# Four decoder blocks on one core: tiles of maxima one or two steps later in each attention, layer norm statistics in two halves

## What is computed

```python
x = x + _L0_xattn_ref(...)          # kernel phase 0
x = x + _L0_ffn_ref(...)            # 1
x = x + _L1_xattn_ref(ctx, ctx, _layernorm(x), mask, Wv, Wk, Wq)      # 2, 16 heads of 16
x = x + _L1_ffn_ref(...)            # 3
x = x + _L2_xattn_ref(_layernorm(x), ctx, ctx, mask, wq, bq, ...)     # 4, 16 heads of 16
x = x + _L2_ffn_ref(...)            # 5
x = x + _L3_xattn_ref(_layernorm(x), ctx, ctx, Wqkv, ..., 32)         # 6, 32 heads of 8
x = x + _L3_ffn_ref(...)            # 7

def _layernorm(x, axis=-1, eps=1e-05):
    return (x - mean(x)) / sqrt(var(x) + eps)

attn = softmax(where(mask == 0, -1e20, q @ k.T / sqrt(EMBED)))        # one head
out = attn @ v
```

## Time and profile before

| | us |
|---|---|
| median of 3 executions | 1696.71 (1695.7 to 1700.76) |
| the profiled execution | 1700.49 |
| its span | 1698.0 |
| TensorE matmul busy | 1474.7 (87%) |
| VectorE busy | 1025.1 (60%) |
| ScalarE busy | 755.2 (44%) |
| GpSimd busy | 116.4 (7%) |

### The profile page before, as it was taken

The page is one execution under the profiler, slowest core; times in us unless marked ns, Lnnn a source line. Parts: engine busy times, 40 slices in busy tenths (PEclk is TensorE's granted clock), DMA queues, the critical chain, the costliest instruction groups (busy, mean ns, idle before and its releaser), DMA issues.

```text
span 1698.0 us, 27047 instructions
## 1 busy us (share of the span) xinstructions
PE 1474.7 (87%) x9938; PEld 1099.3 (65%) x9945; DVE 1025.1 (60%) x2263; ACT 755.2 (44%) x1259; POOL 116.4 (7%) x168
## 2 busy tenths in 40 slices
PE   6999999878879895799889999999997989999456
PEld 4666666556774443477767778787773777778345
DVE  3455564778877764687756162433428888886334
ACT  2222112257764565476752212222214867788223
POOL 1000000000000000111000000000010011010423
PEclk9999999999998997899989999999998999999679
DMA  9451101310000000000009700000100000000176
GB/s 322 140 198 62 62 0 62 135 44 13 13 2 1 1 1 1 24 13 14 2 27 348 237 27 2 2 2 2 32 8 6 1 7 2 7 2 2 45 259 228
DMA packets 59540, 99.82 MB, mean 59 GB/s; under 512 B 10739, under 2 KB 48748, under 8 KB 59246
## 3 DMA queue, kind: packets, MB, share of 16 engines
q1 hardware_dynamic: 57022, 82.57, 14.9%
q10 hardware_dynamic: 512, 11.11, 1.9%
q0 software_dynamic: 1872, 4.27, 0.7%
HBM read 76.23 MB, written 38.35 MB: 67 GB/s over the span
## 4 chain that ended last, share of the span: by engine, by line
PE 49%; issue 22%; DVE 13%; ACT 6%; DVEq 4%; DMA 2%; SPq 2%; ACTq 1%; POOLq 1%; POOL 1%
PE bank L1969 7%; PE bank L1970 7%; PE bank L1645 6%; PE bank L1662 5%; PE bank L2028 3%; PE bank L1768 2%; PE bank L1819 2%; DVE MB L912 2%; DVE plo L930 2%; DMA jx<-copy_routed 2%; PE bank L1739 1%; DVEq L1199 1%; ACT e L1399 1%; PE bank L1741 1%; PE bank L1773 1%
## 5 line engine op out<-in xcount | busy, mean ns | idle before, releaser
L930 DVE TENSOR_TENSOR plo<-e,phi 120x512 f16<-120x512 f32 x256 | 179.7, 707 | 52.1 <-ACT phi L1405 48.4
L1399 ACT ACTIVATE e<-bank 120x512 f32<-120x512 f32 x256 | 150.6, 588 | 42.5 <-PE bank L1773 34.0
L1405 ACT ACTIVATE phi<-e 120x512 f16<-120x512 f32 x256 | 161.3, 630 | 8.8
L912 DVE TENSOR_REDUCE MB<-bank 128x4 bf16<-128x480 f32 x256 | 156.2, 648 | 14.3 <-PE bank L1741 10.4
L1645 PE MATMUL bank<-xT,winT 128*127 128x512 f32 (+1 forms) x256 | 114.8, 594 | 4.7 <-ACTq L1301 4.7
L1662 PE MATMUL bank<-woutT,msk 128*128 128x256 f32 (+1 forms) x512 | 115.2, 379 | 0.0
L1330 ACT ACTIVATE act<-bank,bin 127x512 f32<-127x512 f32 x64 | 43.6, 687 | 151.6 <-DVE dec L749 145.1
L1662 PEld LDWEIGHTS bank<-woutT,msk 128*128 128x128 f32 (+1 forms) x512 | 97.0, 190 | 16.3 <-DVE msk L741 0.3
L1969 PE MATMUL bank<-hah,h1w 128*128 128x512 f32 x256 | 101.3, 396 | 3.3 <-DVE hal L671 3.3
L1768 PE MATMUL bank<-Q_odd,Kpad_odd 128*120 128x256 f16 x512 | 101.8, 281 | 1.1 <-ACT e L1399 1.1
L1768 PE MATMUL bank<-Q_even,Kpad_even 128*120 128x256 f16 x512 | 100.6, 279 | 2.0 <-ACT e L1399 2.0
(11 more groups left out here) (306 smaller groups left out, 3544.8 us busy)
## 6 DMA issues: line engine op xcount, KB each, us to landing
copy_routed<-zeros SPq DMA_DIRECT2D x1, 17028.0 KB
jw<-copy_experts SPq DMA_DIRECT2D x23, 641.0 KB
seen<-in_h1T SPq DMA_DIRECT2D x8, 512.0 KB, 5.7
seen<-in_h2T SPq DMA_DIRECT2D x8, 512.0 KB, 6.4
h1w<-copy_h1T SPq DMA_DIRECT2D x1, 4096.0 KB, 17.1
h2w<-copy_h2T SPq DMA_DIRECT2D x1, 4096.0 KB, 13.9
ctxp<-in_ctxT SPq DMA_DIRECT2D x13, 240.0 KB, 2.7
jx<-copy_routed SPq DMA_DIRECT2D x23, 132.0 KB
```

The costliest lines, as they stand in the source:

```text
L912: dve.tensor_reduce(MB[:, t, h0 // 8, SK + h0 % 8:SK + h0 % 8 + 4], b[:, 0:4 * SK].rearrange("p (h k) -> p h k", h=4), AX.X, ALU.max).then ...
L930: dve.tensor_tensor(plo[:, g % 3, :], e32[:, g % 3, :], phi[:, g % 3, :], ALU.subtract).then_inc(s.lo, 1)
L1399: act.activation(e32[:, g % 3, :], bank[2 + g % 3][0:SK, :], ACT.Exp).then_inc(s.exp, 1)
L1405: act.activation(phi[:, g % 3, :], e32[:, g % 3, :], ACT.Copy).then_inc(s.phi, 1)
```

## The change

Two tables of step numbers and one function. In the first two attentions the tiles of maxima run over steps 4 to 11 where they ran over 3 to 10, two in each; the transposes of the third and fourth quarter move from steps 11 and 12 to 12 and 13. In the third they run over steps 5 to 26 where they ran over 3 to 25 (32 tiles, one or two in a step), and the last transpose moves from step 27 to 28. The statistics of two tiles are made at step `stated`, those of the other two at `stated + 1`, and the semaphore rises after the second half.

```diff
--- before.py
+++ after.py
@@ -54,10 +54,10 @@
         self.approx = TT * heads // 4
         self.quarter = heads // 4
         self.summed = heads == 16
-        self.first, self.last = (3, 10) if heads == 16 else (3, 25)
+        self.first, self.last = (4, 11) if heads == 16 else (5, 26)
         self.turned = (5, 6) if heads == 16 else (6, 8)
         self.projected = (7, 8) if heads == 16 else (10, 12)
-        self.flipped = (9, 10, 11, 12) if heads == 16 else (14, 18, 22, 27)
+        self.flipped = (9, 10, 12, 13) if heads == 16 else (14, 18, 22, 28)
         self.keyed, self.valued, self.columned = heads - 3, heads - 2, heads - 1
         self.lows = (4, 5, 6, 7) if heads == 16 else (4, 6, 8, 10, 12, 14, 16, 18)
         self.split, self.stated, self.normed = (5, 10, 12) if heads == 16 else (5, 20, 23)
@@ -990,6 +990,17 @@
                 dve.wait_ge(s.out, 2 * (L.c0 + i) + h + 1)
                 residual(i, h, bank[7][:, :]).then_inc(s.half if h == 0 else res_done, 1)
 
+            def half_stats(i, h):
+                if h == 0:
+                    dve.drain()
+                for t in (2 * h, 2 * h + 1):
+                    dve.bn_stats(stats[:, t, :], x[:, TT * next_pair(i) + t, :])
+                dve.drain()
+                for t in (2 * h, 2 * h + 1):
+                    last = dve.bn_aggr(mv[:, t, :], stats[:, t, :])
+                if h == 1:
+                    dve.drain().then_inc(ln_var, 1)
+
             mask(0)
             value_rows(0)
             for step in range(-n, PAIRS * n + L.projected[1] + 1):
@@ -1024,7 +1035,9 @@
                     projected(i - 1, L.projected.index(u))
                 if 1 <= i + 2 <= PAIRS and u == L.stated:
                     dve.wait_ge(ln_rstd, 4 * ph + i + 2)
-                    norm_stats(ph, i + 1)
+                    half_stats(i + 1, 0)
+                if 1 <= i + 2 <= PAIRS and u == L.stated + 1:
+                    half_stats(i + 1, 1)
                 if L is L3X and i == PAIRS - 1:
                     if u == 1:
                         route_stats(1)
```

## The result

| | before | change |
|---|---|---|
| median of 10 executions of each, same chip | 1697.11 us (1694.78 to 1702.43) | 1704.34 us (1700.72 to 1708.57) |
| the profiled execution | 1700.49 us | 1702.63 us |
| its span | 1698.0 us | 1700.8 us |
| TensorE matmul busy | 1474.7 us | 1479.6 us |
| mean granted TensorE clock | 0.947 | 0.944 |

The ratio is 1.004 [1.0026, 1.0053]: slower, by about 7 us where +2 was forecast. In a later comparison the same kernel came out at 1.0063 [1.0041, 1.0086] (experiment 9). The time lies inside the range of 1690 to 1704.5 by 0.16 us only; the repeat's median, 1704.74, lies outside it. The case named as likeliest, no difference that can be measured, did not happen.

The account below looks back on a forecast made before the run. No engine bounds the whole; within pairs VectorE and TensorE are near full, so waits count. Terms +4.4, +3.65, -5.7 sum to +2.3, rounded to +2: 1702.5 us profiled, 1698.7 on the median's scale; 8-in-10 range 1690 to 1704.5.

Parts of the forecast that it names:

- The case named as likeliest: Whole kernel: change between -3 and +5 us, within 0.3% and so not measurable as a difference; chance 0.54.
- The lead of 1.1 us in the first attention, 1.0 in the second: Leaving two reductions out of step 3 brings VectorE's later work forward by 1.1 and 1.0 us per pair.
- The later rise of the semaphore: Halved statistics signal GpSimd 1.6 us later on the clock in the first attention, 1.7 in the second; `xln` starts later.
- The wait of ScalarE: Before `xln`, for `nmr`: 4 to 5 us per pair in the first two attentions, total from 30.5 to about 55.
- The fourth copy and the value projection: First attention: copy falls behind `xln`, delaying the value projection 0.95 us in each of two pairs projecting next values.
- The third attention, -5.7: Each of three pairs 2.0 us shorter as `xln` starts earlier, head 0.3 longer: -5.7 us.
- The first rival: All TensorE stops of the third attention come back in full, first two lose as forecast: -7.1 us, 1689.6; chance 0.2.
- The second (no lead kept): Third attention's lead is used up before step 20, `xln` less than 1 us earlier: slower, 1705.7 us; chance 0.22.
- the third (-9 us): The lead grows in the first two attentions too, all three gaining 1 us per pair: about -9, 1687.7; chance 0.04.
- The first two attentions, +8.05: Longer by +4.4 us in the first and +3.65 in the second, from later `xln` and copies.
- The heads: First pairs' preparation, where nothing hides it: 0.6, 0.95 and 0.3 us longer in the three attentions.
- The clock was named as an unknown: TensorE's half-speed stretches after stops may shift: between -2.6 and +2.6 us, taken as nothing.

Follow-up runs that it names:

- experiment 9: The change itself, unaltered, timed once more against the kernel before: 1704.74 us, ratio 1.0063.
- experiment 8: The change, but with the statistics' halves at steps 9 and 10 instead of 10 and 11 in the first two attentions: 1685.02 us, ratio 0.9943 to the kernel before.
- experiment 5: The change, but with `xln` at step 13 instead of 12 in the first two attentions: 1688.13 us, ratio 0.9954 to the kernel before.
- experiment 7: The change, but with third and fourth transposes of maxima kept at steps 11 and 12 in the first two attentions: 1692.64 us, ratio 0.9982 to the kernel before.
- experiment 3: The kernel before, with the whole change in the third attention alone: 1689.58 us, ratio 0.9968 to the kernel before.
- experiment 2: The kernel before with its old tables, but the statistics in two halves in two steps: 1709.03 us, ratio 1.0079 to the kernel before.
- experiment 4: The kernel before, with the whole change in the first two attentions alone: 1704.25 us, ratio 1.0057 to the kernel before.
- experiment 11: The change, but with the second half of the statistics at step 12 instead of 11 in the first two attentions: 1704.7 us, ratio 1.005 to the kernel before.
- experiment 1: The change's new tables, but the statistics whole at step `stated`: 1684.21 us, ratio 0.9927 to the kernel before.
- experiment 6: The change's new tables, statistics whole, `xln` at step 13 instead of 12 in the first two attentions: 1683.81 us, ratio 0.9926 to the kernel before.
- experiment 10: The change's new tables everywhere, but statistics halved in the third attention alone: 1686.01 us, ratio 0.9945 to the kernel before.

## Why the prediction was right, and where it was wrong

- **The lead of 1.1 us in the first attention, 1.0 in the second** is there wherever the new tables are: the exponentials of steps 7 to 10 come 0.8 to 1.1 us earlier in the second pair of the first attention in all ten profiles that have them, and those of steps 5 to 7 0.7 to 1.0 in that of the second. The stop that takes the place of the one for the low queries is the one named, for `low_part`.
- **The later rise of the semaphore.** The statistics took 1.86 us before by their rows (426.03 to 427.89); the 1.95 of the prediction has the gap in front of them in it. Forecast: 1.6 us later on the clock, `xln` at 432.6. Measured: the statistics end 1.51 us later in the pair and `xln` starts 1.15 us later (432.58 - 0.46 for 430.97), as from the end of the aggregates to `xln` there are 2.72 us now and 3.08 before (GpSimd begins 0.11 us behind them for 0.31, its `rstd` takes 1.26 us for 1.04 and its `nmr` 0.20 for 0.57). The wait of ScalarE was forecast at 4 to 5 us in each of the six pairs and at about 55 in total, and is 4.12 to 4.47, and 59.0. Three waits in the third attention (0.97, 0.98 and 1.11 us), which were not there before, are part of the excess. Experiment 8 shows that this place is the price; experiments 5 and 7 that filling the wait gets part of it back.
- **The fourth copy and the value projection.** It begins at 436.13, 0.48 us later in the pair; the forecast was 0.95 (0.91 by its own rows, 436.1 for 435.19). The difference comes from `xln` being less late. In the head of the second attention it waits for the copy, as forecast. The transposes of `xln` behind it start 2.90 us later in the span, where the head's first key product starts 2.20 us later (679.24 for 677.04): 0.70 us is lost there, for 0.95.

```profile
713.17 1.99 PE L1728 MATMUL bank<-wv,ctxp 128*120 128x256 f32 x8 [0.63 <-ACT MBT_even L1404]
...
714.78 1.01 PEld L1587 LDWEIGHTS bank<-ident,xln 128*128 128x128 f32 x8
```

- **The third attention, -5.7.** Measured alone: -5.4. The lead at steps 8 to 10 is 3.0, 1.6 and 2.0 us in the three pairs (forecast 1.8 to 2, more in the first). `xln` starts 1.39 us earlier where 2.0 was forecast, and the pairs are 2.8, 1.3 and 1.0 us shorter for 2.0 each. The first rival (all stops given back, -7.1 us in all) falls: the stop behind the statistics is 0.86 us for 1.91, but that of 2.28 us for the low queries has only changed its place and its cause. The second (no lead kept) falls too, though its time, 1705.7, is close to the one measured: its sign was `xln` less than 1 us earlier. So does the third (-9 us): a gain of that size comes with the new tables only where the statistics stay whole (-12).

```profile
1398.64 0.18 PE L1812 MATMUL bank<-V_odd,phi 120*128 120x18 f16 x1 [2.01 <-DVE plo L930]
```

- **The first two attentions, +8.05.** Measured alone it is +9.7 [+6.4, +12.7]: the forecast lies inside. Pair by pair, in us:

| | first attention | second attention | sum |
|---|---|---|---|
| forecast, pairs in flow | 0.95, 0.95, 1.9 | 0.7, 0, 2.0 | 6.5 |
| change | 0.3, 0.5, 1.9 | 1.3, 0.6, 4.5 | 9.1 |
| change once more (experiment 9) | 1.9, 0.5, 1.9 | 1.3, 0.5, 4.5 | 10.6 |
| change, against experiment 3, which has the code of before here | -1.3, -0.1, 2.6 | 0.0, 2.1, 2.8 | 6.1 |

The heads were forecast 0.6, 0.95 and 0.3 us longer, and are 0.8, 0.6 and -0.2, in experiment 9 0.6, 0.6 and -1.8. Most of the misses are no larger than what two executions of the same code differ by. The largest is the second attention's third pair, +4.5 for +2.0. A stop of 1.96 or 1.97 us is there in all kernels; behind it TensorE has half speed in the change, and the output products take 2.72 us for 1.89. But with the code of before, in experiment 3, they take 3.32 us, so this part of the miss is not the change's:

```profile
826.80 0.17 PE L1805 MATMUL bank<-V_even,phi 120*128 120x17 f16 x1 [1.96 <-DVE plo L930]
...
828.85 2.72 PE L1832 MATMUL bank<-wo,oT 128*128 128x256 f32 x8
```

Before, and experiment 3:

```profile
823.17 0.17 PE L1792 MATMUL bank<-V_even,phi 120*128 120x17 f16 x1 [1.97 <-DVE plo L930]
...
824.63 1.89 PE L1819 MATMUL bank<-wo,oT 128*128 128x256 f32 x8
```

```profile
819.65 0.17 PE L1808 MATMUL bank<-V_even,phi 120*128 120x17 f16 x1 [1.97 <-DVE plo L930]
...
821.36 3.32 PE L1835 MATMUL bank<-wo,oT 128*128 128x256 f32 x8
```

The end of this pair is another matter. There 6.8 us are at half speed in all six profiles in which ScalarE waits for more than 3 us in front of `xln` (the change, experiments 2, 4, 7, 9 and 11), 3.4 us in experiment 5, and none before and in the five others. The change:

```profile
848.00:857.00 9.00, 6.88 (x91) 6.66 (x89) 2.55 (x6) 7.73 (x15) 0.13 (x1) 0.64 0.01 3
```

- **The clock was named as an unknown and taken at nothing**, between -2.6 and +2.6 us. The bound priced one key projection, and the six pairs hold 19 us more at half speed with the change than before. How much of this the change causes is bounded by identical code: in experiment 3 the first two attentions are those of the kernel before, and hold 24 us at half speed where before held 15, over 256.5 us for 253.5. All three profiles with the change's steps there (the change, experiments 9 and 4) hold 31 to 34 us at half speed, in lengths of 262.4 to 264.1 us; the four with new tables and no long wait (1, 6, 8, 10) 3 to 14 us, in 246.8 to 252.3 (added up from each trace's clock over the same six pairs). Experiments 2 and 11, with long waits, hold 27 and 34 us. Experiments 5 and 7 are not in this order: 24 us with a wait of 0.78 us, 17 us with one of 3.39. So half speed tends to go with long waits; that the wait brings it is what fits, and no run changed the clock by itself.
- **What the clock may be worth.** By the clock and the span of every execution the change holds 197 us at half speed and the kernel before 180 (medians over the whole span). Among executions of one and the same kernel 1 us more of it goes with 0.2 us more time (133 executions, compared within their kernel and comparison). By that the 17 us more would be an estimated 3.4 us; the most that they can be is half, 8.5 us, as products at half speed take about twice as long (3.40 us for 1.84 in experiment 8).
- **What stays open**: experiments 5 and 7 fell 9 and 6 us further below the change than their traced pairs, of which their heads make up 3.5 and 3.9 us. Profiles are single executions, in which pairs of identical code already differ by 1.7 us, and the stretch before the first attention by 4.0.

So the sum of +2.3 is short of the measured +6.8 [+4.4, +9.0] by 4.5 us. Of these 1.65 lie in the term of the first two attentions and 0.3 in that of the third, each within its interval, and 2.5 in neither part alone. Each term agrees with its measurement, the whole does not, and no run shows which term is short; the likeliest is the clock that was taken at nothing, as its estimated 3.4 us would bring the sum to 5.7. The order of what pays and what is paid was right: the lead, the later rise, the wait in front of `xln` and the gain of the third attention are all there. The size put the result on the wrong side of the 5 us that can be told from nothing, and that the time still lies inside the range is luck. **The better kernel** is the one with the new tables and the statistics whole: 0.9927 [0.9912, 0.9942].

## What to carry to other kernels

When an operation is split so that its first half fits a gap, look at what waits for the last half, and count everything that its engine now does between the halves as delay of the consumer. Here the same two halves one step earlier come out 16 to 20 us below those of the change (0.9943 for 1.004 and 1.0063). Behind an engine that executes in order a wait is paid by all that is queued there: either move the producer up or put ready work ahead of the waiting instruction, and test the parts of a change apart, since a part that gains 12 us may lie under one that loses 19.

## What was not expected of the hardware

- Stops of the same length are followed by half speed or by full. In experiment 5 TensorE stands 2.19 us at the place where it stands 2.18 in the change, and the eight key products behind it take 1.84 us there and 3.40 here:

```profile
425.98 0.17 PE L1805 MATMUL bank<-V_odd,phi 120*128 120x17 f16 x1 [2.19 <-DVE plo L930]
426.49 1.84 PE L1714 MATMUL bank<-ctxp,bdk 128*128 128x240 f32 x8
```

- In the head of the third attention the 16 key products took 5.98 us before, 6.27 in the change, 4.78 in its repeat, and 3.46 in experiments 1 and 6: the same products, in the same kernel too, at different speed.
- GpSimd's `rstd` took 1.04 us before and in experiments 1 and 8, and 1.26 us in the change. VectorE works beside it in all of these, before too at low parts, so what makes the difference is not shown.
